# Routing 6250 rows to experts: batches of four tiles against batches of up to eight, with the first batches' order written out

## What is computed

```python
xn = _layernorm(x, axis=-1)
x = x + gnn(xn, edge_weight, src, dst) + mix(xn[None], ...)[0]
# the expert block, on _layernorm(x):
logits = jnp.einsum('bsd,de->bse', xn, Wr) + br
top_vals, top_idx = jax.lax.top_k(logits, 2)
w = jax.nn.softmax(top_vals, axis=-1)
for e in range(8):
    h = gelu(xn @ W1[e] + b1[e]);  y_e = h @ W2[e] + b2[e]
    y = y + y_e * w_full[..., e, None]
x = x + y
```

## Time and profile before

| | |
|---|---|
| median of 3 runs | 1101.61 us (1101.25 to 1101.87) |
| the profiled execution | 1099.49 us, its span 1097.6 us |
| busy, share of the span | TensorE 87%, VectorE 66%, ScalarE 57%, GpSimd 57% |
| chain that ended last, largest lines | experts' matmuls L1842 and L1852 8% each, L1439 5%, scatters L652 3% |
| experts' first tile load starts | 643.49 us |

### The profile page before, as it was taken

How to read it: one execution, slowest core, us unless ns; L and a number is a source line. 1 busy time by engine, 2 the same in 40 slices (tenths; PEclk the granted TensorE clock), 3 DMA queues, 4 the chain that set the end, 5 groups by cost and what they waited for, 6 DMA issues and landing times.

```text
span 1097.6 us, 26629 instructions
## 1 busy us (share of the span) xinstructions
PE 957.1 (87%) x6320; PEld 820.4 (75%) x6321; DVE 726.9 (66%) x2600; ACT 624.1 (57%) x1771; POOL 624.3 (57%) x1088
## 2 busy tenths in 40 slices
PE   3957977989999999999898549999999799999996
PEld 2635657888888888888775339899899777777775
DVE  4844475878888888888768834444444466666664
ACT  4538644667776777767448735555555344444442
POOL 2892376666666776766427725766522354544444
PEclk9988998999999999999999869999999899999998
DMA  8322213631000100023125544434322123222321
GB/s 234 79 25 81 64 21 92 199 97 28 16 16 16 27 19 16 16 19 26 17 63 194 195 112 129 135 119 120 103 74 63 56 89 91 88 87 79 96 85 53
DMA packets 64618, 86.19 MB, mean 79 GB/s; under 512 B 17895, under 2 KB 52676, under 8 KB 64318
## 3 DMA queue, kind: packets, MB, share of 16 engines
q1 hardware_dynamic: 44661, 43.16, 14.7%
q0 software_dynamic: 18944, 40.84, 13.3%
q10 hardware_dynamic: 966, 1.74, 0.5%
HBM read 54.18 MB, written 33.01 MB: 79 GB/s over the span
## 4 chain that ended last, share of the span: by engine, by line
PE 20%; issue 10%; DVE 9%; DVEq 7%; POOL 3%; DMA 2%; SPq 0%; POOLq 0%; ACT 0%; ACTq 0%
PE banks L1842 8%; PE banks L1852 8%; DVEq L1439 5%; POOL send_d L652 3%; DVE R L1476 2%; DVE R L1484 2%; PE banks L1794 1%; PE banks L1833 1%; DMA R<-send_d 1%; DVE dest_now L1450 1%; DMA out_dram<-R,dest_now 1%; DVE R L1343 1%; DVE R L1462 0%; DVE R L1487 0%; DVE get_now L1444 0%
## 5 line engine op out<-in xcount | busy, mean ns | idle before, releaser
L1842 PE MATMUL banks<-R 128*128 128x128 f32 x1696 | 213.7, 280 | 12.6 <-issue 7.8
L1842 PEld LDWEIGHTS banks<-R 128*128 128x128 f32 x1696 | 201.6, 195 | 18.1 <-issue 12.9
L1852 PE MATMUL banks<-R 128*128 x848 | 201.5, 381 | 0.0
L939 ACT ACTIVATE R<-banks,bet_c,gam_c 128x128 f32<-128x128 f32 x212 | 85.4, 453 | 159.1 <-PE banks L1833 156.9
L949 ACT ACTIVATE R<-banks,b1c 128x128 f32<-128x128 f32 x424 | 132.1, 364 | 70.6 <-PE banks L1842 70.3
L1852 PEld LDWEIGHTS banks<-R 128*128 128x128 f32 x848 | 154.3, 192 | 16.5
L1462 DVE COPY R<-R 128x1024 f32 x106 | 74.1, 699 | 82.0 <-PE banks L1842 41.8
L652 POOL DMA_INDIRECT send_d<-R,slot_all x98 | 96.5, 985 | 49.0 <-issue 40.8
L1666 PE MATMUL banks<-R 128*128 128x126 f32 (+5 forms) x768 | 106.7, 283 | 10.1 <-ACT R L841 10.1
L1666 PEld LDWEIGHTS banks<-R 128*128 128x128 f32 x768 | 98.0, 195 | 22.9 <-ACT R L841 21.2
L665 POOL DMA_INDIRECT first_d<-R,dest_now x54 | 59.0, 1093 | 96.6 <-DVE R L1468 86.9
(11 more groups left out here) (321 smaller groups left out, 1850.4 us busy)
## 6 DMA issues: line engine op xcount, KB each, us to landing
R<-send_d SPq DMA_DIRECT2D x106, 131.0 KB, 2.2
R<-in_L_ffn_W_dram SPq DMA_DIRECT2D x16, 512.0 KB, 4.7
R<-in_x_dram SPq DMA_DIRECT2D x14, 512.0 KB, 3.9
R<-in_x_dram SPq DMA_DIRECT2D x5, 1024.0 KB, 21.7
rec_d<-R SPq DMA_DIRECT2D x1, 3125.0 KB
send_d<-zrow SPq DMA_DIRECT2D x14, 131.0 KB, 7.7
send_d<-R,slot_all POOLq DMA_INDIRECT x98
R<-incl_d,R POOLq DMA_INDIRECT x80
```

The costliest lines, as they stand in the source:

```text
L939: last = nc.scalar.activation(xmT[b][:, kb * P:(kb + 1) * P], bank[b][:, kb * P:(kb + 1) * P], ACT.Identity, bias=bet_c[:, kb:kb + 1], sca ...
L1842: last = mm(bank[2 + 2 * b + c // 2][:, (c % 2) * P:(c % 2 + 1) * P], w1c[b][:, kb, c * P:(c + 1) * P], xmT[b][:, kb * P:(kb + 1) * P], st ...
L1852: last = mm(bank[6 + b][:, 0:D], hT[b][:, c, :], w2s[:, bass.ds(e, 1), c, :].rearrange("p a h -> p (a h)"), start=(c == 0), stop=(c == H / ...
```

## The change

The groups get the sizes 1, 4, 4, 8, 8, 8, 8, 4, 4. `group`, `first_tile` and `half_of` follow the sizes; x is still loaded in blocks of four tiles, and `block_of` gives a half's block. `sum_rows` adds a half's raw logits at once and frees its PSUM buffer there (`x2_done`); ScalarE's `norms(q)` waits for that count instead of `std_need`. The one-hot matrices stand at the end of `ohb`, which has room for nine, and some small tiles move into the region R4. The first batches' order is written out on VectorE and TensorE; the loop after them places batch q - 1 behind the sums of batch q + 1. GpSimd and ScalarE keep their order.

```diff
-            def sum_rows(q, nt=4, r=P):
...
-                xl(last)
-                dve.sem_inc(S["std_need"], 1)
...
+            def sum_rows(q, nt, r=P):
+
+                at = first_tile(q)
+                for h in range((nt + 1) // 2):
+                    block, inside = block_of(q, h)
+                    b, m, at2 = block % 2, min(2, nt - 2 * h), at + 2 * h
+                    dve.wait_ge(S[f"xt{b}"], (block // 2) * 16 + 16)
                     dve.wait_ge(S["x2_psum"], half_of(q, h) + 1)
...
+                    now = raw[0:r, q % 2, 2 * h:2 * h + m, :]
+                    TT(now, now, ps[0:r, 0:m, D:D + NX], ALU.add).then_inc(S["x2_done"], 1)
...
+        SIZES = (1, 4, 4) + (2 * 4,) * ((FULL - 16) // 8) + (4, 4)
+        MOST = max(SIZES)
+        NG = len(SIZES)
...
+        def block_of(q, h):
+
+            return (1 + (first_tile(q) + 2 * h) // 4, 2 * h % 4) if q else (0, 0)
...
             def norms(q, nt=4, r=P):
 
-                act.wait_ge(S["std_need"], q + 1)
+                act.wait_ge(S["x2_done"], half_of(q + 1, 0))
...
             sum_rows(0, *group(0))
-            for q in range(NG12 + 1):
-                if q < NG12:
+            sum_rows(1, *group(1))
+            norm_scales(0, *group(0))
+            choose(0, *group(0))
+            sum_rows(2, *group(2))
+            place_rows(0, *group(0))
+            norm_scales(1, *group(1))
+            choose(1, *group(1))
+            place_rows(1, *group(1))
+            sum_rows(3, *group(3))
+            norm_scales(2, *group(2))
+            choose(2, *group(2))
+            for q in range(3, NG):
+                if q + 1 < NG:
                     sum_rows(q + 1, *group(q + 1))
+                place_rows(q - 1, *group(q - 1))
                 norm_scales(q, *group(q))
-                if q > 0:
-                    place_rows(q - 1, *group(q - 1))
                 choose(q, *group(q))
             dve.sem_inc(S["wexp_need"], 1)
...
-                mm(bank[6][:, 0:5 * 2 * NR], trib[:, :], ohb[:, :, :].rearrange("p t e -> p (t e)"), start=True, stop=False)
-                for t in range(4):
...
+                mm(bank[6][:, 0:(nt + 1) * 2 * NR], trib[:, :], ohb[:, at:MOST + 1, :].rearrange("p t e -> p (t e)"), start=True, stop=False)
+                for t in range(nt):
...
-            sum_pe(0, 0)
-            sum_pe(1, 0)
-            sum_pe(1, 1)
-            for q in range(NG12 + 1):
-                if q + 2 <= NG12:
-                    sum_pe(q + 2, 0)
-                if q + 2 <= NG12:
-                    sum_pe(q + 2, 1)
+            def sums_pe(q):
+                for h in range((SIZES[q] + 1) // 2):
+                    sum_pe(q, h)
+            sums_pe(0)
+            sums_pe(1)
+            sums_pe(2)
+            rank_pe(0)
+            for h in range(SIZES[3] // 2):
+                sum_pe(3, h)
+                if h == 2:
+                    rank_pe(1)
+            for q in range(2, NG):
+                if q + 2 < NG:
+                    sums_pe(q + 2)
                 rank_pe(q)
```

More of the change, by code:

```diff
@@ L162, in gnn_layer @@
         xt = [late(4, D) for _ in range(2)]
-        squares = late(4, D)
+        squares = late(8, D)
         PT, lam = [squares[:, 2 * i:2 * i + 2, :] for i in range(2)]
+        late.at = 18 * D
+        sel, slot18 = [late(8, 2 * NR) for _ in range(2)]
+        lg, top = late(8, NX), late(8, 8)
+        topi = late(8, 8, dt=U32)
+        assert late.at <= 20 * D
         moe = Carve(R2)
@@ L230, in gnn_layer @@
         csum = sb("csum", [P, KB])
[L231 to L240, removed]
+        scl = sb("scl", [P, 2, 8])
+        shift = sb("shift", [P, 2, 8])
+        raw = sb("raw", [P, 2, 8, NX])
+        ohb = sb("ohb", [P, 9, 2 * NR], BF16)
+        slotf = sb("slotf", [P, 8, 2])
         base18 = sb("base18", [P, 2 * NR])
@@ L334, in over_tiles @@
             return v.rearrange("p (a d) -> p a d", a=1).broadcast_to([v.shape[0], nt, v.shape[1]])
+        SIZES = (1, 4, 4) + (2 * 4,) * ((FULL - 16) // 8) + (4, 4)
+        MOST = max(SIZES)
+        assert sum(SIZES) == NT and FULL % 8 == 0
+        NG = len(SIZES)
         def half_of(q, h):
-            return 2 * q - 1 + h if q else 0
+            return sum((n + 1) // 2 for n in SIZES[:q]) + h
         def group(q):
-            return (4, P) if q else (1, TAIL)
+            return (SIZES[q], P) if q else (1, TAIL)
         def first_tile(q):
-            return 4 * (q - 1) if q else FULL
+            return sum(SIZES[1:q]) if q else FULL
+        def block_of(q, h):
+            return (1 + (first_tile(q) + 2 * h) // 4, 2 * h % 4) if q else (0, 0)
         BATCH = ((0, 4), (4, 16), (16, 32), (32, NT))
@@ L654, in send_row @@
                     in_=row_all[0:r, t, :], in_offset=None).then_inc(S["next_sent" if c else "top_sent"], 16)
-            for q in range(NG12 + 1):
+            for q in range(NG):
                 pool.wait_ge(S["z_ready"], q + 1)
                 pool.wait_ge(S["slot_ready"], q + 1)
-                for t in range(first_tile(q), min(first_tile(q) + 4, NT)):
+                for t in range(first_tile(q), first_tile(q) + SIZES[q]):
                     send_row(t, 0)
@@ L1329, in _, with norm_scales @@
             dve.wait_ge(S["tables"], 1)
-            def sum_rows(q, nt=4, r=P):
[L1334 to L1338, removed]
+            def sum_rows(q, nt, r=P):
[4 more added lines that the diff above has]
+                    dve.wait_ge(S[f"xt{b}"], (block // 2) * 16 + 16)
                     dve.wait_ge(S["x2_psum"], half_of(q, h) + 1)
                     ps = sums[half_of(q, h) % 3]
[L1341 to L1344, removed]
-                xl(last)
-                dve.sem_inc(S["std_need"], 1)
[L1347 to L1351, removed]
+                    TT(raw[0:r, q % 2, 2 * h:2 * h + m, :], ps[0:r, 0:m, D + NX:AVG],
+                       stdv[0:r, at2:at2 + m].rearrange("p (t a) -> p t a", a=1).broadcast_to([r, m, NX]), ALU.mult)
+                    TT(row_all[0:r, at2:at2 + m, 0:D], ps[0:r, 0:m, 0:D], xt[b][0:r, inside:inside + m, :], ALU.add)
+                    xl(TT(row_all[0:r, at2:at2 + m, MEAN], ps[0:r, 0:m, AVG], mv[0:r, at2:at2 + m, 0], ALU.add))
+                    now = raw[0:r, q % 2, 2 * h:2 * h + m, :]
+                    TT(now, now, ps[0:r, 0:m, D:D + NX], ALU.add).then_inc(S["x2_done"], 1)
+            def norm_scales(q, nt, r=P):
                 dve.wait_ge(S["std_done"], q + 1)
@@ L1358, in norm_scales, with choose @@
                     .then_inc(S["scl_ready"], 1)
-            def choose(q, nt=4, r=P):
+            def choose(q, nt, r=P):
+                dve.wait_ge(S["x2_done"], half_of(q + 1, 0))
+                at = MOST - nt
                 v = raw[0:r, q % 2, 0:nt, :]
@@ L1376, in choose, with place_rows @@
                 dve.sem_inc(S["msk_ready"], 1)
-            def place_rows(q, nt=4, r=P):
+            def place_rows(q, nt, r=P):
+                at = MOST - nt
                 dve.wait_ge(S["rank_psum"], q + 1)
@@ L1382, in place_rows @@
                       over_tiles(base18[0:r, :], nt), ALU.add))
-                TT(base18[:, :], bank[6][:, 4 * 2 * NR:5 * 2 * NR], base18[:, :], ALU.add)
-                xl(TT(sel[0:r, 0:nt, :], ohb[0:r, 0:nt, :], slot18[0:r, 0:nt, :], ALU.mult))
+                TT(base18[:, :], bank[6][:, nt * 2 * NR:(nt + 1) * 2 * NR], base18[:, :], ALU.add)
+                xl(TT(sel[0:r, 0:nt, :], ohb[0:r, at:MOST, :], slot18[0:r, 0:nt, :], ALU.mult))
                 xl(nc.vector.tensor_reduce(slotf[0:r, 0:nt, :].rearrange("p t c -> p (t c)"),
@@ L1389, in _ @@
             sum_rows(0, *group(0))
-            for q in range(NG12 + 1):
-                if q < NG12:
+            sum_rows(1, *group(1))
[10 more added lines that the diff above has]
+            for q in range(3, NG):
+                if q + 1 < NG:
                     sum_rows(q + 1, *group(q + 1))
+                place_rows(q - 1, *group(q - 1))
                 norm_scales(q, *group(q))
-                if q > 0:
-                    place_rows(q - 1, *group(q - 1))
                 choose(q, *group(q))
             dve.sem_inc(S["wexp_need"], 1)
-            place_rows(NG12, *group(NG12))
+            place_rows(NG - 1, *group(NG - 1))
             tl = chain(dve, S["t_own"])
```

15 lines of the change are left out of this document (8 added, 7 removed).

## The result

The changed kernel takes 1112.58 us (median of 6 runs, 1110.39 to 1116.12), the kernel before 1101.74 us in the same comparison. The ratio is 1.0093 with a 95% interval of 1.0069 to 1.0116: slower by 0.9%, where 1112.5 us was forecast. The profiled execution took 1111.14 us, with a span of 1109.3 (before 1097.6).

The account below looks back on a forecast made before the run. GpSimd's row scatters were taken to bound the router, the last one releasing the expert stage. Tile 8 +12.47 us and the steps behind it -1.54 gave +10.9, on 1101.61 us a time of 1112.5; range 1108.8 to 1117.

Parts of the forecast that it names:

- The last scatter sets the end: Router's end: the first expert load follows the landing of GpSimd's last scatter, so moving it moves the whole expert stage.
- The reordering gains nothing: First slots: place_rows(1) ahead of sum_rows(3) waits 2.3 us for TensorE; first scatter at 576.65 against 576.60 before.
- place_rows(2) behind sum_rows(4): VectorE's queue: slots of tiles 4 to 7 wait for eight tiles' sums, until 589.84; GpSimd gets a hole of 8.9 us.
- Prices of the eight-tile forms: VectorE: on the line through one and four tiles, place_rows costs 1.20 us and choose 3.05; one half of sums 1.08.
- rival (b): VectorE's eight-tile forms cost nearer twice four: tile 8 1.9 us later, rounds 11.1 us, time about 1117; chance 0.06.
- Tile 8 +12.5: GpSimd: the scatter of tile 8 starts at 599.82 instead of 587.35, 12.5 us later.
- Rival (a): TensorE's clock falls in the idleness at 575 to 577, half of sums 2.1 us longer: 1114.7 to 1116.8; chance 0.15.
- granted clock 1.00 at 577 to 580: Sign to look for in the changed kernel's profile: TensorE keeps its full clock at 577 to 580 us.
- The 39 steps -1.5: GpSimd from tile 8 on: scatters at their own pace, 51.1 us to the last one's end instead of 52.64.
- The landing: Last scatter's landing: taken as 3.67 us, possibly up to 1.5 us shorter with the pads out of its way.
- The expert stage unchanged: Sign to look for in the changed kernel's profile: the expert stage behind the last scatter keeps its length.
- the two holes: GpSimd idle for about 9 us from 581.7 and 4 us from 595.7, then steps of 1.27 us without waits.

Follow-up runs that it names:

- Experiment 1: Changed kernel with TensorE's count matmuls of batch 1 behind two halves of batch 3 instead of three; ratio 1.0063 to the kernel before.
- experiment 7: Changed kernel with count matmuls 1 behind two halves of batch 3, each place_rows behind two halves of the next sums; ratio 1.0063 to the kernel before.
- the place alone: Kernel before with place_rows(q - 1) moved between the two halves of sum_rows(q + 1), signal unchanged; ratio 0.9995.
- both edits: Kernel before with place_rows(q - 1) between sum_rows(q + 1)'s halves and the one-hot matrices' last instruction signalling TensorE itself; ratios 0.9952 and 0.9963.

## Why the prediction was right

Point by point, by its own steps:

- *The last scatter sets the end.* Right: over these fourteen profiled executions the span less the start of the last scatter is 456.3 to 459.6 us, while that start moves by 15 us.
- *The reordering gains nothing* because count matmuls 1 stand behind three halves: right. VectorE waited 2.45 us (2.3 forecast), tile 0 at 575.99 (576.65 forecast from a router start 0.54 later). Experiment 1 shows the other side.
- *place_rows(2) behind sum_rows(4)*: right. slot_all of tiles 4 to 7 at 590.45 + 0.17 (589.84 forecast), the hole 10.60 instead of 8.9; the forecast counted it without the step of 0.3 between two scatters.
- *Prices of the eight-tile forms*: choose 3.10 us (590.85 to 593.95 in the changed kernel's VectorE rows), 3.05 forecast; place_rows 1.19 (598.39 to 599.58), 1.20 forecast. The line through one and four tiles held; rival (b) is out. One half of sums cost 0.96 (575.09 to 576.05), not 1.08: the wait that I had read off a single row is shorter when only one add follows it. It hardly shows, since these halves follow TensorE.
- *Tile 8 +12.5*: measured +13.1 in absolute time, +13.6 from the router's start. The missing 1.2 is the clock's fall, 1.7, less about 0.5 for four cheaper halves (0.12 each). **Rival (a) had too low a chance**, 0.15: its condition came true in both executions of the changed kernel, so the sign "granted clock 1.00 at 577 to 580" failed. Its price was 2.1 and is 1.7, since the fall came only when the half had begun.
- *The 39 steps -1.5*: measured -2.3 to the start of the last scatter. The pace of 1.265 was right; the gap of 0.42 at a group's start, which I had charged at each of five groups, does not show at any group behind tile 8 (0.30 as everywhere).
- *The landing*, 3.67 taken with 1.5 less as a bound: 2.48. *The expert stage unchanged*: 2.1 us longer in this execution, 1 of it beside a later rise of the clock, the rest open.

So the agreement of 1112.6 with 1112.5 is better than its terms, and to the tenth it is luck. A hidden +1.2 at tile 8 and +2.1 in the experts stand against -0.8 in the steps, -1.2 in the landing and -0.5 in the router's start. The range had kept the landing and the clock; the steps, the router's start and the expert stage stood in none of its terms. What is not luck is the path: the two holes, their places and their releasers came as forecast, and tile 8 within 1.2 us.

The Trainium skill ("Perfetto Trace Analysis", section "Optimizing Scalar/DVE Operations") says that grouping can improve throughput where the engine is saturated. The traces agree on VectorE's throughput, 9.04 us for a round of eight (slot_all 590.45 to 599.49) against 10.5 for two rounds of four. That throughput was not what this stage ended in: its end hung on how early the first slots came.

## What to carry to other kernels

When one engine consumes what a chain of others produces in batches, write down for each batch its ready time plus the consumer's time for all that remains: the largest of these sums is the end, and filling any other hole is worth nothing. A larger batch pays only where the consumer has more queued than the longer round takes. At the first eights it had four rows, 5.1 us, against 9; from tile 8 on it had eight, 10.1 us, and there the eights did save 2.3 us. And before a step is moved up in one queue, look where its input stands in the other queues: one position in TensorE's queue undid the move, and removing one wait of 0.2 us in the producer's round, which brought it under the consumer's pace, gained 3.0 us where the batching lost 11.3.

## What was not expected of the hardware

- TensorE's granted clock fell from 1.00 to 0.50 after an idle time of 2.11 us, in both executions of the changed kernel and in the run with the place of batch 2 earlier, although one of 2.57 us had left it alone in the kernel before. The length of an idle time does not by itself tell whether the clock falls.
- It also fell at the router's start in four of the fourteen executions (experiment 7, the place alone, both edits twice). TensorE had been idle four times shortly before, for 1.0, 0.47, 0.42 and 0.63 us, and the ten executions that kept 1.00 show the same four idle times, to 0.01 us. A fall costs 1.7 us and shifts every start behind it, so an experiment's trace is worth a look at the clock ahead of the edited code.
- At the start of the expert stage the clock rose 4.0 us after the first matmul in the kernel before and 6.6 us after it in the changed one.
- The last scatter lands in 2.48 us in the changed kernel and in 3.67 before. Over the fourteen executions it took 2.43 to 2.60 us in the nine where the last write of the pads was issued over 3 us ahead of it, and 2.80 to 3.83 in the five where that was 1.5 us or less. No run moves the pads alone.
